# Slots of two rebuilt attentions: made for half a batch by dense products, or made per step by depth-32 selection products

## What is computed

```python
q, k, v = split(lora_linear(x, w_attn, b_attn, la_attn, lb_attn))   # att0; att1: xn @ Wqkv + bqkv
att = einsum('bhqd,bhkd->bhqk', q, k) / sqrt(8)
att = where(causal, att, -inf)                                       # att0 only
y = einsum('bhqk,bhkd->bhqd', softmax(att), v)
x = x + lora_linear(y, w_proj, b_proj, la_proj, lb_proj)             # att1: y @ Wo + bo
```

## Time and profile before

| | |
|---|---|
| median of 3 runs | 1085.1 us (1082.22 to 1087.16) |
| the profiled execution | 1085.6 us, of which its span, first to last instruction, 1083.8 us |
| mean granted TensorE clock | 0.911 of full speed |
| TensorE products busy | 973.4 us, 90% of the span |
| VectorE / ScalarE busy | 631.6 us (58%) / 528.5 us (49%) |
| att0, from its first tile to its last product | 13.31 to 150.87 us of the span |
| att1, the same | 589.03 to 728.24 us of the span |

### The profile page before, as it was taken

How to read it: one execution, slowest core, us unless ns; L and a number is a source line. 1 busy time by engine, 2 the same in 40 slices (tenths; PEclk the granted TensorE clock), 3 DMA queues, 4 the chain that set the end, 5 groups by cost and what they waited for, 6 DMA issues and landing times.

```text
span 1083.8 us, 19401 instructions
## 1 busy us (share of the span) xinstructions
PE 973.4 (90%) x6750; PEld 749.1 (69%) x6750; DVE 631.6 (58%) x1505; ACT 528.5 (49%) x1103; POOL 106.2 (10%) x174
## 2 busy tenths in 40 slices
PE   5998878999999999999998788879999888888898
PEld 2554557888888888888886344548999765555665
DVE  5555547566665666655655656433222399999774
ACT  3354345555555555555542345325444366666541
POOL 2000120000000000000002100000000044444100
PEclk9698769999999999999998767558999999999997
DMA  6000000000000000000001000000110000000000
GB/s 235 1 2 1 1 1 1 1 2 1 0 0 0 0 0 0 0 0 0 0 0 40 1 1 1 1 1 10 41 56 29 1 1 0 0 0 0 2 19 19
DMA packets 6411, 12.69 MB, mean 12 GB/s; under 512 B 481, under 2 KB 2529, under 8 KB 5985
## 3 DMA queue, kind: packets, MB, share of 16 engines
q1 hardware_dynamic: 6368, 12.13, 3.4%
HBM read 11.60 MB, written 0.52 MB: 11 GB/s over the span
## 4 chain that ended last, share of the span: by engine, by line
PE 73%; DVE 14%; issue 5%; ACT 4%; POOL 1%; DVEq 1%; DMA 1%; SPq 0%; ACTq 0%
PE psum L880 8%; PE psum L892 8%; PE psum L1014 6%; PE psum L860 4%; PE psum L861 4%; PE psum L862 4%; PE psum L852 4%; DVE arena L1746 4%; PE psum L603 3%; PE psum L845 3%; PE psum L582 3%; PE psum L518 3%; PE psum L546 2%; PE psum L998 2%; PE psum L999 2%
## 5 line engine op out<-in xcount | busy, mean ns | idle before, releaser
L1869 DVE TENSOR_REDUCE xnegmax<-psum 128x1 f32<-128x768 f32 x128 | 122.3, 956 | 139.3 <-PE psum L862 139.0
L1395 ACT ACTIVATE arena<-psum,xnegmax 128x768 f32<-128x768 f32 x128 | 115.4, 902 | 139.0 <-DVE xnegmax L1869 97.7
L1623 DVE TENSOR_REDUCE negmax<-psum 128x6 f32<-128x768 f32 (+1 forms) x64 | 69.7, 1090 | 86.3 <-PE psum L546 43.5
L880 PE MATMUL psum<-pack_a,arena 128*128 128x128 f32 x768 | 106.8, 275 | 0.2 <-ACT arena L1386 0.2
L860 PE MATMUL psum<-kv_high,xq_high 128*128 128x384 f32 x256 | 100.7, 393 | 3.3 <-DVE xq_low L1858 1.7
L880 PEld LDWEIGHTS psum<-pack_a,arena 128*128 128x128 f32 x768 | 87.3, 141 | 13.9 <-issue 12.3
L1386 ACT ACTIVATE arena<-psum 128x512 f32<-128x512 f32 x128 | 75.9, 593 | 42.5 <-PE psum L880 42.5
L892 PE MATMUL psum<-arena,xv 128*64 128x256 f32 x768 | 90.0, 383 | 0.0
L1207 ACT ACTIVATE pT<-psum 128x768 f32<-128x768 f32 (+1 forms) x64 | 58.7, 917 | 57.0 <-PE psum L586 34.5
L862 PE MATMUL psum<-kv_high,xq_low 128*128 128x384 f32 x256 | 86.5, 338 | 0.0
L861 PE MATMUL psum<-kv_low,xq_high 128*128 128x384 f32 x256 | 86.5, 338 | 0.0
(11 more groups left out here) (272 smaller groups left out, 1902.6 us busy)
## 6 DMA issues: line engine op xcount, KB each, us to landing
w1b<-in_w SPq DMA_DIRECT2D x9, 256.0 KB, 2.8
w2b<-in_w SPq DMA_DIRECT2D x9, 256.0 KB, 2.7
pack_v<-in_pack_v SPq DMA_DIRECT2D x1, 1088.0 KB, 9.1
pack_l<-in_pack_l SPq DMA_DIRECT2D x1, 1079.5 KB, 12.0
pack_q<-in_pack_q SPq DMA_DIRECT2D x1, 1024.0 KB, 6.9
pack_a<-in_pack_a SPq DMA_DIRECT2D x1, 657.0 KB, 6.0
x<-in_x SPq DMA_DIRECT2D x2, 256.0 KB, 3.1
arena<-in_mask SPq DMA_DIRECT2D x1, 512.0 KB, 3.6
```

The lines of the kernel that those rows point to most:

```text
L880: last = transpose(bank[4 + (3 * u + c) % 2][:, (2 * i + h) * P:(2 * i + h + 1) * P], xprob[:, u % 2, h * KEYS + kt * P:h * KEYS + (kt + 1 ...
L1395: activation(xprob[:, u % 2, half * KEYS:(half + 1) * KEYS].rearrange("p (c w) -> p c w", c=2), src, ACT.Exp, bias=xnegmax[:, u % 2, half: ...
L1623: v.tensor_reduce(negmax4[:, 2 * p:2 * p + 2, 0:blocks], psum[:, 2:4, 0:a.width].rearrange("p a (c k) -> p a c k", c=blocks), AX.X, ALU.ma ...
L1869: v.tensor_reduce(xnegmax[:, u % 2, half:half + 1], banks_pair(half), AX.XY, ALU.max, negate=True)\
```

## The change

The parts are split once and spread over the rows afterwards.

- **q and k once per half.** `queries_keys(h, kind)` is one product per kind and half (4 an attention) with the plain weights. `high` (ScalarE) and `low` (VectorE) split each into a rounded part and its remainder, `split`. For the first half this stands in the prologue; for the second half TensorE has transposes at the end of step 1, q at 2, k at 3, values at 4.
- **Slots per step.** `spread_slots(i+1, 1)`: four products with 0/1 selection weights, on the 32 rows of the group's heads, 256 columns each, two for the query slots and two for the key slots, all in bank 1. ScalarE takes them out in two instructions (`slots`). `qslot` and `kslot` now hold three groups, not a half.
- **Two banks per pair of scores.** `scores(i,0)` uses banks 2 and 3, `scores(i,1)` banks 6 and 7. `scores(i,1)` moves ahead of `transposed_scores(i-1,0)`. The results of `weighted` go to the other half of bank 0, and their emptying (`results`) from three steps behind to two.
- **Way out, one piece a step.** Each step ends with at most one extra piece in bank 1; `evacuated` makes the next step's `spread_slots` wait until that bank is emptied. For batch element b the pieces are half of the transposes, the other half, `back`, `project`, at steps 4b+6 to 4b+9. `STEPS` is 18.
- **Smaller things.** `wslot`, `fill_slots`, `slot_weights` and most of the clearing on GpSimd are gone; `v_aug4` has a stride of 9 and is filled by four VectorE instructions a half instead of one; a table `spread` (256 KB) is loaded after pack a and rounded on ScalarE ahead of the mask; context normalisation has other steps.

```diff
+SLOT_PARTS = ((0, 1, 0), (2, 2, 3))
+PARTS = 4
-        TILE_STEP = {2: 0, 3: 1, 4: 6, 5: 7, 6: 8, 7: 9}
-        TOKEN_STEP = {0: 10, 1: 13, 2: 15, 3: 18}
-        STEPS = GROUPS + 3
+        HALF_T, HALF_Q, HALF_K, HALF_V, EFFECTIVE = 1, 2, 3, 4, 5
+        TOKEN_STEP = {b: G * b + G + 2 for b in range(B)}
+        STEPS = GROUPS + 2
+        SCORE_BANKS = ((2, 3), (6, 7))
+            sp.dma_start(spread_in[:, :], spread_d).then_inc(loaded["s"], 16)
...
             # TensorE
+                def queries_keys(h, kind, bk):
+                    mm(bank[bk][:, :], w[:, kind * D:(kind + 1) * D], zT[:, h * BANK:(h + 1) * BANK], ...)
+                def spread_slots(it, bk):
+                    h, b, g = it // (2 * G), it // G % 2, it % G
+                    r = slice(HG * HD * g, HG * HD * (g + 1))
+                    a.wait(pe, "low", 2 * h + 2)
+                    for part in range(PARTS):
+                        last = mm(bank[bk][:, part // 2 * T:(part // 2 + 1) * T], spread_of[r, part, :],
+                                  split[r, h, part, b * T:(b + 1) * T], start=(part == 0), stop=(part == PARTS - 1), ...)
                 def scores(it, p):
                     if p == 0:
-                        a.wait(pe, "slot_ready", 2 * (it // (2 * G) * G + g) + 2)
+                        a.wait(pe, "slot_ready", it + 1)
                     if it:
-                        a.wait(pe, "max_done", 2 * it + p)
+                        a.wait(pe, "max_done", 2 * it + p - 1)
...
                 for i in range(STEPS):
                     if i < GROUPS:
                         scores(i, 0)
                     if 1 <= i <= GROUPS:
                         shifted(i - 1)
-                        transposed_scores(i - 1, 0)
                     if i < GROUPS:
                         scores(i, 1)
-                    if 2 <= i <= GROUPS + 1:
+                    if i + 1 < GROUPS:
+                        evacuated(i - 1)
+                        spread_slots(i + 1, 1)
+                    if 1 <= i <= GROUPS:
+                        transposed_scores(i - 1, 0)
+                    if i >= 2:
                         weighted(i - 2)
                     if 1 <= i <= GROUPS:
                         transposed_scores(i - 1, 1)
+                    if i + 1 < GROUPS:
+                        a.wait(pe, "slot_ready", i + 2)
+                    else:
+                        evacuated(i - 1)
+                    # then at most one piece in bank 1: transposes, q, k, values, effective projection, way out
...
             # ScalarE
+                def high(h, kind, bk):
+                    a.wait(act, "qk_psum", 2 * h + kind + 1)
+                    activation(split[:, h, 2 * kind, :], bank[bk][:, :], ACT.Identity, bias=(bias_q, bias_k)[kind])
+                def slots(it, bk):
+                    a.wait(act, "spread_psum", it + 1)
+                    activation(kslot[:, it % 3, :], bank[bk][:, T:2 * T], ACT.Identity, bias=col("a", "unit_rows"))
+                    activation(qslot[:, it % 3, :], bank[bk][:, 0:T], ACT.Copy).then_inc(heads["slot_ready"], 1)
...
                 for i in range(STEPS):
                     if 1 <= i <= GROUPS:
                         shifted(i - 1)
+                        exponentials(i - 1, 0)
+                    if i + 1 < GROUPS:
+                        slots(i + 1, 1)
-                    if i >= 3:
-                        results(i - 3)
+                    if i >= 2:
+                        results(i - 2)
                     if 1 <= i <= GROUPS:
                         exponentials(i - 1, 1)
...
             # VectorE
+                def low(h, kind, bk):
+                    a.wait(dve, "high", 2 * h + kind + 1)
+                    v.scalar_tensor_tensor(split[:, h, 2 * kind + 1, :], bank[bk][:, :], (bias_q, bias_k)[kind],
+                                           split[:, h, 2 * kind, :].bitcast(f32), ALU.add, ALU.subtract)
```

More of the change, by code:

```diff
@@ new lines, in evacuated @@
+                def evacuated(step):
+                    if step == HALF_T:
+                        a.wait(pe, "zT_act", 2)
+                    elif step in (HALF_Q, HALF_K):
+                        a.wait(pe, "low", step - HALF_Q + 3)
+                    elif step == HALF_V:
+                        a.wait(pe, "v_ready", 2)
+                    elif step == EFFECTIVE and a is att0:
+                        pe.wait_ge(prep_dve, 2)
+                    elif step >= TOKEN_STEP[0]:
+                        b, piece = divmod(step - TOKEN_STEP[0], 4)
+                        if piece < 2:
+                            a.wait(pe, "tok_ready", 2 * b + piece + 1)
+                        else:
+                            a.wait(pe, ("yT_ready", "added")[piece - 2], b + 1)
@@ L545, in scores @@
                                 out, keys = slice(u * T, (u + 1) * T), T
-                            last = mm(bank[2 + k][:, out], qslot[r, g, at + u * P:at + (u + 1) * P],
-                                      kslot[r, g, at:at + keys], start=(u == 1 or not a.causal), stop=not a.causal,
+                            last = mm(bank[SCORE_BANKS[p][k]][:, out], qslot[r, it % 3, u * P:(u + 1) * P],
+                                      kslot[r, it % 3, 0:keys], start=(u == 1 or not a.causal), stop=not a.causal,
                                       skip_group_check=True)
@@ new lines, in head_attention @@
+                    if i == HALF_T:
+                        wait_normed(pe, name, 1)
+                        for t in range(4):
+                            last = transpose(bank[1][:, t * P:(t + 1) * P], src[:, 4 + t, :], ident)
+                        last.then_inc(heads["zT_psum"], 1)
+                    if i in (HALF_Q, HALF_K):
+                        a.wait(pe, "zT_act", 2)
+                        queries_keys(1, i - HALF_Q, 1)
+                    if i == HALF_V:
+                        values(1, 1)
@@ new lines, in head_attention @@
+                    if i == EFFECTIVE and a is att0:
+                        effective_projection()
+                    if i >= TOKEN_STEP[0]:
+                        b, piece = divmod(i - TOKEN_STEP[0], 4)
+                        if piece < 2:
+                            to_tokens(b, piece)
+                        elif piece == 2:
+                            back(b)
+                        else:
+                            project(b)
+                evacuated(STEPS - 1)
+                for u in range(2):
+                    to_tokens(B - 1, u, (1, 2)[u])
@@ L701, in cross_operands @@
+                back(B - 1)
+                project(B - 1)
             def cross_operands():
@@ L2096, in att0_aside @@
             def att0_aside(i):
[L2097 removed]
+                for work, steps in ((centre, (5, 7, 9, 11)), (variances, (6, 8, 10, 12)), (scale, (8, 10, 12, 14))):
                     for c, step in enumerate(steps):
@@ L2343, in _arrange @@
     arrays = {f"pack_{key}": np.concatenate([c[n] for n, _ in columns], 1) for key, columns in LAYOUT.items()}
+    spread = np.zeros((G, HG, HD, PARTS, HG, ROWS), np.float32)
+    for parts in SLOT_PARTS:
+        for s, part in enumerate(parts):
+            for j in range(HG):
+                spread[:, j, np.arange(HD), part, j, s * HD + np.arange(HD)] = 1.0
+    arrays["spread"] = spread.reshape(P, PARTS * P)
     arrays["x"] = f("x")
```

363 lines of the change are left out of this document (137 added, 226 removed).

## The result

The kernel after takes 1068.1 us (median of 4 runs, 1065.5 to 1071.6), the kernel before, run beside it on the same chip, 1083.7 us (1080.4 to 1087.2). The ratio is 0.9858, 95% interval 0.9811 to 0.9905: shorter by 1.4%, clear of the noise. The forecast was 1073 us. In the experiments, executions of one kernel differ by up to 33 us and go with the mean granted clock (experiment 3: 1025.5 us at 0.947, 1044.5 at 0.917), so a median there is of all executions, while a ratio leaves the slow ones out unless said otherwise.

What follows compares the result with a forecast made beforehand. TensorE was taken as the bound, its step length set by the tiles and the granted clock. Middles -4.0 and +1.6, starts -1.6 and -0.9, tails -2.5 and -5.3 sum to -12.7 from 1085.6: 1073 us, range 1050 to 1096.

Steps and rivals of the forecast that it cites:

- Plain step of att0: att0's step without an extra piece at the full clock: from 4.51 us before to 4.8 us after.
- Slow step of att0: att0's step without an extra piece at the slow clock: from 7.01 us before to 7.6 us after.
- Step of att1: att1's step without an extra piece: 4.3 us at full clock, where ScalarE decides, and 6.1 us at the slow clock.
- Extra pieces: Transposes, q, k, values, effective weights and way out in the 14 steps: 10 us at full clock, 19 at the slow one.
- The slow share of att0: One third of att0's 14 middle steps at the slow clock, giving 92.6 us, a change of -4.0.
- The slow share of att1: Three quarters of att1's 14 middle steps at the slow clock, giving 95.2 us, a change of +1.6.
- clock-up rival: Clock stays up: slow share one sixth in att0, a quarter in att1; -37.8, 1047 us; chance 0.20.
- Tails: Ends of both attentions, with four transposes instead of a projection, eight transposes and two waits: -2.5 att0, -5.3 att1.
- Starts: Beginnings of both attentions, with weight copies and four tiles gone and selection products added: -1.6 us att0, -0.9 att1.
- serial products: Rival: selection products run one after the other with their weights, 0.86 us full, 1.5 or more slow; 1091 us; chance 0.12.
- The evacuation of the slots: Rival: slot emptying behind the exponentials on ScalarE bounds; half a us in 28 steps, +14, 1087 us; chance 0.14.
- Clock down: Rival: 85% of att0's steps and all of att1's at the slow clock; +23, 1108 us; chance 0.14.

Runs made afterwards that it cites:

- experiment 3: Kernel after with ScalarE's squares of the contexts and of the next normalisation in both attentions one step later: 1035.4 us (1025.5 to 1044.5).
- experiment 11: experiment 7 plus three unread dense products in each gap of both attentions' starts: 1018.2 us, ratio to before 0.9374.
- 5: Kernel after with only the contexts' squares and their variances one step later: 1045.6 us, ratio to before 0.9617.
- 6: Kernel after with only the next normalisation's squares one step later, in both attentions: 1058.3 us, ratio to before 0.9608.
- (1): Kernel after with the four selection products of every step issued twice into the same bank: 1097.2 us; ratio to before 1.0133 for three of four runs.
- experiment 4: Kernel after with two more unread dense products in each of steps 1 to 14 of both attentions: 1061.1 us (1050.2 to 1068.8).
- experiment 10: Kernel after with two way-out pieces, back and project, in one step: 1068.0 us, ratio to before 0.9822.
- 12: experiment 11 plus two more unread dense products in each of steps 1 to 14 of att1: 1021.3 us, ratio to before 0.9412.
- experiment 7: experiment 3 plus att1's second normalisation half finished in steps 0 and 1, and both attentions' last scale behind the last two tokens: 1032.5 us.

## Why the prediction was right in its sum, and where it was not

- **Plain step of att0:** 4.8 us forecast. Step 5 takes 4.62 at 1.00 with the effective weights in it, which I had at 0.3 more, so 5.1. The set of selection products was put at 0.55 and is 0.47, and the gap is gone. The new wait for the first exponentials is there:

```profile
53.94 0.30 PEld L604 LDWEIGHTS psum<-qshift,kslot 32*128 32x128 f32 x4 [0.38 <-ACT pT L1224]
```

  The 0.38 us is the idle time of the weight loads. TensorE's products of `weighted` begin at 52.97 and these at 53.94, 0.97 us apart for 0.79 before, so the wait costs 0.18 us for the 0.3 forecast.
- **Slow step of att0:** 7.6 without a piece, so about 8.6 with one token piece; 8.08 measured. The selection products cost 0.86, not 1.05.
- **Step of att1:** 4.3 forecast at full clock, where I let ScalarE decide, and 3.76 measured. ScalarE was no bound. At the low clock `back` makes 6.34, against 6.1 + 0.6.
- **Extra pieces:** about right, and it was the step without them that I had too dear. In experiment 3 att1 runs at 1.00 from 598.4 to 622.3 us. These are its step without a piece, with one token piece, with `back` and with `project`:

```profile
599.24:603.00 3.76, 3.46 (x41) 2.29 (x39) 3.17 (x7) 2.57 (x6) 0.00 (x0) 1.00 0.00 0
603.00:607.31 4.31, 4.05 (x46) 2.69 (x44) 3.00 (x6) 3.71 (x7) 0.00 (x0) 1.00 0.02 6
611.61:615.70 4.09, 3.84 (x43) 2.47 (x41) 2.87 (x5) 3.01 (x7) 0.00 (x0) 1.00 0.01 2
615.70:620.89 5.19, 4.94 (x49) 3.37 (x48) 2.83 (x5) 3.83 (x8) 0.00 (x0) 1.00 0.02 3
```

  They add 0.55, 0.33 and 1.43 us, for 0.52, 0.3 and 1.65 forecast. A step of att0 with one token piece takes 4.87 (76.16:81.03 above), which by 0.55 leaves about 4.3 without it, an estimate, for 4.8. All 14 steps of att0 at the full clock were forecast at 76.7 us and take 71.6 in experiment 11.
- **The slow share of att0, the step that failed:** one third of the steps forecast, clock 0.65 measured. At 0.65 the engine is slow for 70% of the time; with steps about 1.7 times as long that is some 58% of the steps. On my own prices this share gives 0.42 x 76.7 + 0.58 x 124.5 = 104 us for 92.6, an error of +12, of which cheaper steps gave 5 back. The sentence behind it was "Those waits go too". They went in TensorE's own order, but side work that the diff had moved on ScalarE and VectorE put new ones there (0.58 us at step 8), and behind the first the clock fell. I had named the condition (clock under 0.7 in att0) for being wrong in this part.
- **The slow share of att1:** three quarters, measured 0.62 in the clock, 76% of the time and near two thirds of the steps. Here the price was the larger error: on my own prices two thirds give 92.3 us, so it was about 6.5 us of the 9.5 that the middle came out below the forecast.
- **My reading of before's clock was wrong.** I wrote that it fell in att0 when the way out brought waits such as the 1.18 us. It fell at 98.6 us, and that wait ended at 105.19. Nor was the stretch at 1.00 ahead of it free of stalls, and not everything else was TensorE's own queue: it had the waits of 0.47, 0.70 and 0.88 us shown with experiments 3, 5 and 6. So "no stall holds it" had no support in these rows.
- **Two sums are off by 0.2 us:** 14 x 4.3 + 10 - 0.5 is 69.7 and 14 x 6.1 + 19 - 0.9 is 103.5, and the clock-up rival's 1085.6 - 37.8 is 1047.8. Nothing rests on it.
- **Tails:** -2.5 and -5.3 forecast, -2.2 and -5.4 measured, with waits of 2.64 and 2.40 us in them that could have been saved.
- **Starts:** att0 -1.2 for -1.6. Att1 +0.2 for -0.9: the first maxima waited behind the side work of VectorE, 2.97 us for TensorE. The time between the attentions fell by 1.9 us; I had taken it as unchanged and have not traced that.
- **The rivals:** serial products are refuted (1). The evacuation of the slots is no bound: no wait of more than 0.9 us for qslot, and outside the starts one of 0.18. Clock down was half true in att0. Clock up in att0 is what the same change gives once ScalarE isn't held up (0.91 over its 14 steps in experiment 3); att1's stayed at 0.79 there, and the whole 1035 us for the rival's 1047. Both were on the list as states of the clock; what decides between them in att0, the place of the contexts' four squares, was not.

So the sum was right by luck in part, because errors of opposite sign met: +6.5 us in att0's middle, -9.5 in att1's.

## What to carry to other kernels

When a change moves side work in an in-order queue, price each move by the instruction that stands next behind it: a square waiting 1.6 us for its centring held up the one operand that TensorE needed. Where TensorE is the bound and its granted clock falls easily, a short wait may matter by more than its length: here one of 0.58 us stood ahead of 61 us at half the clock, while others as long cost only themselves. Look in the trace for the last wait ahead of each fall of the clock, and test it by removing it before you call it the cause; several falls here had no wait ahead of them. Compare versions by the same step at the same clock before trusting totals, since the totals differ by 30 us between executions of one kernel.

## What the runs showed of the hardware that was not expected

- Four products of 32 rows by 256 columns in one row group, each with its own weights, add 0.47 us at 2.4 GHz and 0.86 us at 1.2 GHz, 0.12 and 0.215 us each. Of the dense products of 512 columns three have a record of 0.97 us and two (experiment 4, at 56.86) one of 0.73, so 512 columns add 0.24 us at 2.4 GHz, twice the 0.12. The time goes with the columns, and next to nothing is left for the loads of the weights.

```profile
22.19 0.97 PE L663 MATMUL psum<-split,identr 128*128 128x512 f32 x3
```

- An engine without gaps did not bring the clock back: in after TensorE's records covered 61.50 of 61.50 us at 0.50. With two dense 128-row products more in each step it came back after 17 us. That these did it is not shown, as it also came back after 24 us in experiment 10, without them.
- Products that nobody reads, placed in gaps of 0.84 to 0.96 us, kept the clock up in att0's first steps in one of two profiles (11, not 12) and shortened the slow stretch at att1's start in both, to 6.8 and 10.2 us from 20.5 in experiment 7.
